# A graph attention scores pass: gather indices copied by GpSimd instead of ScalarE, and step words loaded once per engine

## The reference, as far as it matters

```
q, k, v = x @ Wq.T + bq, x @ Wk.T + bk, x @ Wv.T + bv
score[edge, head] = sum over d of q[src, head, d] * k[dst, head, d]
```

## Time and profile before

| | |
|---|---|
| median of 3 timed runs | 3451.3 us (3447.9 to 3469.26) |
| span of the profiled execution, first to last instruction | 3661.6 us |
| what lies around that span | not listed |
| granted TensorE clock, mean over the span | 0.899 |
| the scores pass in that execution | about 168 to 947 us |
| PE, DVE, ACT, POOL busy over the span | 2959.8, 2114.3, 1131.1, 1144.8 us |
| DMA over the span | 477.37 MB, mean 130 GB/s |

### The profile page before, as it was taken

How to read it: one execution, slowest core, us unless ns; L and a number is a source line. 1 busy time by engine, 2 the same in 40 slices (tenths; PEclk the granted TensorE clock), 3 DMA queues, 4 the chain that set the end, 5 groups by cost and what they waited for, 6 DMA issues and landing times. The chain is left out here.

```text
span 3661.6 us, 59295 instructions
## 1 busy us (share of the span) xinstructions
PE 2959.8 (81%) x12458; PEld 2278.7 (62%) x12459; DVE 2114.3 (58%) x4039; ACT 1131.1 (31%) x2511; POOL 1144.8 (31%) x1257
## 2 busy tenths in 40 slices
PE   3766566666289969999999799999997996667878
PEld 2633344433155537777776688888886885555677
DVE  6356555555689754434522465656667995885521
ACT  1010111100188723333333000000004994655412
POOL 3155555555022110000000455555552002760033
PEclk9877787866599989999999899999998998998979
DMA  1587777777377610000000665656662114005334
GB/s 47 176 251 218 213 226 224 225 227 223 90 228 226 181 70 1 1 8 8 5 4 8 202 192 173 191 173 188 191 188 67 44 44 153 1 1 183 101 130 136
DMA packets 259676, 477.37 MB, mean 130 GB/s; under 512 B 31340, under 2 KB 148020, under 8 KB 258156
## 3 DMA queue, kind: packets, MB, share of 16 engines
q1 hardware_dynamic: 198510, 282.91, 24.4%
q0 software_dynamic: 61056, 193.06, 18.4%
HBM read 376.68 MB, written 100.16 MB: 130 GB/s over the span
## 5 line engine op out<-in xcount | busy, mean ns | idle before, releaser
L1664 PE MATMUL bank<-conv_w,conv_eT 128*128 128x256 f32 x2520 | 579.7, 380 | 0.0
L1605 POOL DMA_INDIRECT conv_h<-table_h,conv_ix x424 | 416.3, 982 | 339.0 <-ACT conv_ix L1594 191.1
L1664 PEld LDWEIGHTS bank<-conv_w,conv_eT 128*128 128x128 f32 x2520 | 480.2, 191 | 65.8
L557 POOL DMA_INDIRECT x<-table_qv,scores_ix x324 | 307.2, 948 | 393.1 <-ACT scores_ix L505 280.8
L579 PE MATMUL bank<-scores_k,scores_hotT 128*128 x864 | 327.7, 518 | 53.3 <-issue 48.7
L1397 ACT ACTIVATE area<-bank,nodes_bi,nodes_sc 128x320 f32<-128x320 f32 x320 | 197.6, 617 | 373.9 <-PE bank L1314 373.9
L579 PEld LDWEIGHTS bank<-scores_k,scores_hotT 128*128 128x128 f32 x864 | 205.6, 258 | 136.6 <-issue 105.2
L571 PE MATMUL bank<-lines,pick 128*128 x216 | 74.8, 346 | 256.3 <-DVE scores_hotT L662 150.8
L1545 DVE SCALAR_TENSOR_TENSOR x<-bank,nodes_w,x 128x256 f32<-128x256 f32 x200 | 96.6, 484 | 319.9 <-PE bank L1323 319.9
L505 ACT ACTIVATE scores_ix<-src 128x2 int32 x216 | 43.8, 203 | 727.1 <-DVE scores_qk L669 429.0
L1045 PE MATMUL bank<-attend_pv,rows 128*128 128x260 f32 x864 | 237.9, 405 | 36.7 <-DVE attend_pv L1026 21.5
(11 more groups left out here) (449 smaller groups left out, 5445.7 us busy)
## 6 DMA issues: line engine op xcount, KB each, us to landing
conv_eT<-in_edges SPq DMA_DIRECT2D x212, 384.0 KB
attend_v<-edge_v SPq DMA_DIRECT2D x216, 256.0 KB, 3.0
edge_v<-x SPq DMA_DIRECT2D x162, 256.0 KB
edge_v<-scores_qv SPq DMA_DIRECT2D x54, 256.0 KB
hidden_rows<-top_wide SPq DMA_DIRECT2D x25, 512.0 KB, 3.2
projected<-spline_hst SPq DMA_DIRECT2D x10, 960.0 KB, 4.5
ball_hT<-projected SPq DMA_DIRECT2D x5, 1920.0 KB, 17.3
top_wd<-in_top_wd SPq DMA_DIRECT2D x8, 1024.0 KB, 13.7
```

The lines of the kernel that those rows point to most:

```text
L557: nc.gpsimd.indirect_dma_start(out=qv(u)[:, g - u * G, :], out_offset=None, in_=m.d_qv, in_offset=bass.IndirectOffsetOnAxis(ap=ix[:, g:g + ...
L1605: nc.gpsimd.indirect_dma_start(out=h[:, u, g, :], out_offset=None, in_=m.d_h, in_offset=bass.IndirectOffsetOnAxis(ap=ix[:, u * G + g:u * G ...
L1664: mm = nc.tensor.matmul(banks[u][:, g * F:(g + 1) * F], eT[:, u, g, c], w[:, c], start=c == 0, stop=c == EC - 1)
```

## The change

The index copy moves from ACT to POOL. POOL now loads and decodes the step's word itself, waits for the free slot, copies the indices, waits for its own copy, and issues the gathers. ACT keeps only the copies for the projection and the context and one new wait (for its own exponentials).

On PE and DVE each step's word is loaded once and kept in registers until its second use: PE keeps 4 words, DVE 3, carried from round to round (`carried`, `words`). The node tile and the edge tile are decoded where they are used, and only the one that is used; SP and POOL decode only the edge tile. DVE drops three waits: for `k_made` before the one-hot, for `reduced` before the product, and for `scored` before the reduction.

```diff
             @block.scalar
-                act.sem_inc(freed, RING)
-                def sources(r, u):
-                    s = act.snap(r * RING + u)
-                    t, i = step_at(act, m, s)
-                    act.wait_ge(freed, s + 1)
-                    nc.scalar.activation(ix[:, u * G:(u + 1) * G], m.src[:, bass.ds(i, G)], ACT.Copy).then_inc(index, 1)
...
                 with act.Fori(0, FIRST) as n:
-                    for u in range(RING):
-                        sources(n + 1, u)
-                        if u % 2:
-                            j = u // 2
-                            act.wait_ge(product, n * 4 + (j + 1))
+                    for j in range(2 * FT):
+                        act.wait_ge(product, n * 4 + (j + 1))
...
+                act.wait_ge(exps, FT)
                 with act.Fori(0, SECOND) as n:
+                    for u in range(2):
+                        take_tile(n * 2 + u)
+                        keep_front(n * 2 + u, u)
...
             @block.gpsimd
+                pool.sem_inc(freed, RING)
                 with pool.Fori(0, rounds_of(pool, m, RING)) as r:
                     for u in range(RING):
-                        pool.wait_ge(index, r * RING + (u + 1))
+                        s = pool.snap(r * RING + u)
+                        i = edge_tile(pool, word_at(pool, m, s))
+                        pool.wait_ge(freed, s + 1)
+                        nc.gpsimd.tensor_copy(ix[:, u * G:(u + 1) * G], m.src[:, bass.ds(i, G)]).then_inc(index, 1)
+                        pool.wait_ge(index, s + 1)
                         pool.wait_ge(stored[u], r * 16 + 16)
...
             @block.tensor
-                def spread_out(r, u):
-                    t, i = step_at(pe, m, r * RING + u)
+                def spread_out(r, u, word):
+                    i = edge_tile(pe, word)
...
-                def keys(r, u):
-                    t, i = step_at(pe, m, r * RING + u)
+                def keys(r, u, word):
+                    t = node_tile(pe, word)
...
+                def round_of(r, words, between):
+                    for u in range(RING):
+                        keys(r, u, words[u])
+                        words.append(word_at(pe, m, r * RING + (u + KEPT)))
...
             @block.vector
-                def one_hot(r, u):
-                    t, i = step_at(dve, m, r * RING + u)
+                def one_hot(r, u, word):
+                    t = node_tile(dve, word)
                     dve.wait_ge(spread, r * RING + (u + 1))
-                    dve.wait_ge(k_made, r * RING + (u + 1))
...
-                    dve.wait_ge(reduced, r * RING + (u + 1))
...
+                        if more or u + 3 < RING:
+                            words.append(word_at(dve, m, r * RING + (u + 3)))
...
-                    dve.wait_ge(scored, r * RING + (u + 1))
...
-                    t, i = step_at(dve, m, r * RING + u)
```

More of the change, by code:

```diff
@@ L625, in _ @@
                 with pe.Fori(0, SECOND) as n:
[L626 to L634, removed]
+                    for x, word in zip(carried, round_of(n + (FIRST + SHIFT), [pe.snap(x) for x in carried], lambda u: mixing(n, u))):
+                        pe.reg_mov(x, word)
+                rounds(FIRST + SHIFT + SECOND, last)
                 front(NT - 1)
+                words = [pe.snap(x) for x in carried]
                 for u in range(RING):
-                    keys(last, u)
+                    keys(last, u, words[u])
+                    if u + KEPT < RING:
+                        words.append(word_at(pe, m, last * RING + (u + KEPT)))
                     if u + UN - 1 < RING:
-                        spread_out(last, u + UN - 1)
+                        spread_out(last, u + UN - 1, words[u + UN - 1])
                 back(NT - 1, 0)
@@ L684, in _, with round_of @@
-                last = last_round(dve, m, RING)
-                for u in range(2):
-                    t, i = step_at(dve, m, u)
-                    dve.wait_ge(spread, u + 1)
-                    nc.vector.tensor_scalar(hotT[:, u % UN], numbers(u), m.node[:, bass.ds(t, 1)], None, ALU.is_equal).then_inc(hots, 1)
-                with dve.Fori(0, FIRST + 1) as r:
-                    for u in range(RING):
-                        score(r, u, True)
+                def round_of(r, words, more):
+                    for u in range(RING):
+                        for g in range(u * G, (u + 1) * G):
+                            dve.wait_ge(gathered[g], r * 16 + 16)
+                        dve.wait_ge(k_made, r * RING + (u + 1 + UN))
+                        nc.vector.tensor_tensor(qk[:, u % 2].rearrange("p (g f) -> p g f", g=G), qv(u)[:, :, 0:F],
+                                                banks[u % UN][:, 0:G * F].rearrange("p (g f) -> p g f", g=G), ALU.mult).then_inc(freed, 1)
+                        if more or u + 3 < RING:
+                            words.append(word_at(dve, m, r * RING + (u + 3)))
+                        if u + 2 < RING:
+                            one_hot(r, u + 2, words[u + 2])
+                        elif more:
+                            one_hot(r + 1, u + 2 - RING, words[u + 2])
+                        i = edge_tile(dve, words[u])
+                        dve.wait_ge(freed, r * RING + (u + 1 + RING))
+                        nc.vector.tensor_reduce(dot[:, u % 2], qk[:, u % 2].rearrange("p (g h d) -> p g h d", g=G, h=HEADS),
+                                                AX.X, ALU.add).then_inc(reduced, 1)
+                        dve.wait_ge(reduced, r * RING + (u + 3))
+                        dve.wait_ge(scored, r * RING + (u + 2))
+                        at = m.scores[:, :, bass.ds(i, G)]
+                        nc.vector.tensor_tensor(at, at, dot[:, u % 2].rearrange("p g h -> p h g"), ALU.add).then_inc(scored, 1)
+                    return words[RING:]
@@ new lines, in rounds @@
+                def rounds(begin, end):
+                    with dve.Fori(begin, end) as r:
+                        for x, word in zip(carried, round_of(r, [dve.snap(x) for x in carried], True)):
+                            dve.reg_mov(x, word)
+                last = last_round(dve, m, RING)
+                carried = [dve.alloc_register(f"scores_word{j}") for j in range(3)]
+                for u in range(3):
+                    word = word_at(dve, m, u)
+                    dve.reg_mov(carried[u], word)
+                    if u < 2:
+                        one_hot(0, u, word)
```

85 lines of the change are left out of this document (29 added, 56 removed).

## The result

| | before | after |
|---|---|---|
| median of 4 runs each, us | 3456.11 (3447.9 to 3469.26) | 3602.91 (3599.96 to 3629.96) |
| ratio | 1 | 1.0437 (95% interval 1.0407 to 1.0467) |
| span of the profiled execution, us | 3661.6, again 3452.1 | 3598.3 |

The change makes the kernel 4.4% slower, 146.8 us between the medians. Forecast were 3581 us, within 3425 to 3640. One timed execution of the kernel before, taken beside the first experiments, lasted 14303 us; why is not known, and no ratio here counts it.

A forecast was written before the change was run, and what follows sets the result against it. Untraced, POOL's gathers were taken to be close to the pace of the scores pass. That pass going from 604 to 734 us cost 130, all other parts 0: 3451.3 + 130 = 3581 us, range 3425 to 3640.

The forecast's parts named there:

- the sequencer can't issue the next gather until the copy is done: Scores pass: POOL's queue runs empty once a step; 0.83 us from copy end to the gather that waited.
- asked for as a sign: Profile after: pairs of gathers 1.25 us apart, successive pairs 3.3; DVE's waits for gathers from 25 us to a hundred or more.
- The cycle: POOL's step in the scores pass after the change: 3.22 us plus a gap of 0 to 0.30, taken as 3.30.
- The tail: Scores pass after the change: 21 us from the last gather to the stage's end.
- The pass before: Untraced scores pass before the change: 569 to 734 us, taken as 604 with five sixths of the trace's surplus in it.
- DVE at 2.2 us a step is quicker: Scores pass before the change: DVE's 2.2 us a step is under POOL's 2.50, so POOL is close to the pace.
- The span: Profiled execution after the change: 3620 to 3720 us, as DVE's slowed steps already take longer than POOL's 3.3.
- The edits at nothing: ACT's lost copies, DVE's and PE's single loads, the dropped waits and SP's fewer decodes: 0 us each.
- A: Rival: DVE's slow stretches in the scores pass are real and hide POOL's 3.3 us; 3440 us, no change; chance 0.17.
- B: Rival: word loads cause DVE's issue gaps in the scores pass, making it 78 us shorter; 3373 us; chance 0.13.
- C: Rival: same mechanism, 0.30 us gap before the copy, whole surplus in the scores pass; 3663 us; chance 0.05.
- D: Rival: POOL's sequencer queues gathers behind the copy without waiting; cycle 2.8 us, cost 22 us, 3473 us; chance 0.07.

The follow-up runs named there:

- e1: The kernel before with only the index copy moved to POOL, words still loaded twice: 3595.54 us, ratio 1.0387; run again, 3594.66 us.
- e4: The changed kernel with POOL copying the next step's indices before issuing this step's gathers: 3457.68 us, ratio 1.0019 to the kernel before.
- e2: The changed kernel with the index copy back on ACT, sparing loads and dropped waits kept: 3443.52 us, ratio 0.9971 to the kernel before; again, 0.9988.
- e7: The changed kernel with POOL copying two steps' indices, waiting once, then issuing four gathers: 3530.75 us, ratio 1.0212 to the kernel before.
- e3: The changed kernel with gathers reading a table filled once, each copy waited for eight steps later: 3447.8 us, ratio 0.9978 to the kernel before.
- e6: The kernel before plus one 128x25 operation per step on DVE, between the reduction and the add: 3455.65 us, ratio 1.0006.
- after_again: The changed kernel, unaltered, run a second time: 3613.45 us, ratio 1.0438 to the kernel before.

## Why the prediction was right

**The mechanism holds.** The step "the sequencer can't issue the next gather until the copy is done" is shown from both sides: e1 has the whole loss of the pass without the other edits, e4 with the copy but without waiting for a fresh one loses 13.7 us of gathers against e2 where after loses 163.9, and e7 with half the waits loses half. What was asked for as a sign is there: pairs of gathers 1.28 apart, successive pairs 3.26 to 3.27 apart, no longer run, and 203.3 us of waits for gathers on DVE.

**The cycle.** Forecast was 3.22 us and a gap, taken as 3.30. The gap before the copy is nothing (gather 302.72 + 0.95, copy 303.68), the other terms 0.03 to 0.04 more, and the typical cycle 3.26. That the mean is 3.300 all the same is luck: it comes from four steps of 4.85 to 4.87 us and from 3.32 to 3.34 at the end of most rounds, which I hadn't thought of. 0.83 from the earlier trace rows, a single row of a different releaser, is the price again (0.83, 0.84, and 0.89 at times).

**The tail was mis-sized.** "21 behind the last" was carried over from before, where the ring was full and DVE up to eight steps behind the gathers. A starved DVE follows closely: from the last gather (881.3) to 2.7 us behind the last product's start (889.3), which is where the pass ended at 947 in the first profile, are 10.7 us. The pass after is 724 us, not 734.

**The pass before was mis-sized.** "I put five sixths of the surplus in this pass, so 604." By the same ends it is 583 us (168 to 751): all but 14 us of the 210.3 sat in it, and the bound of 569 was nearer than my value. The cost in the pass is 724 - 583 = 141 us for the forecast 130. With 6 us in the next stage that I had at nothing, the difference is 147, as measured. The remaining 5 of the 22 us between 3581 and 3602.9 are the medians of before themselves, 3451.3 and 3456.1. The sum of 561 us for this pass came to 22 us too little because it had POOL's gathers follow each other without a stop. "DVE at 2.2 us a step is quicker" is the reading behind it, and it wasn't borne out: 2.2 is one of the shortest steps, and the mean in the undisturbed profile is 2.58. This did no harm to the forecast, as POOL's 3.26 is slower than either.

**The span was wrong.** I expected 3620 to 3720 for the profiled execution, from the reading "that the trace hides it behind a slowed DVE". Span and timed runs agree within 2 us in every later profile (3598.3 us of an execution of 3599.96, and 3452.1 of 3453.79). The slow register instructions belonged to that one execution. That they weren't the kernel's usual pace was right; that every profile brings them was not, as no later one has such a surplus. What brought them is open.

**The edits at nothing.** ACT's relief shows no gain: e1 and e4 have it, and neither is faster than before. The sparing loads bring 14 us in the pass where POOL can use them (e2) and none beside the waiting POOL (711.0 in e1, 710.8 in after), as "with POOL at 3.3 us a step DVE and PE have a microsecond to spare" says. POOL's own load is hidden, though it isn't 0.3 us but 0.62 in the median: the copy still starts as the gather ends. The Trainium skill (DMA: Bandwidth & Descriptors, section Latency and other measured facts) gives about 600 ns as the floor of a register load. By that rule an exposed load a step would cost 130 us, an estimate from the page's figure; on POOL beside gathers the median of 622 ns is close to it, though its shortest load took 283 ns, and on DVE (304 ns in the median) the trace contradicts it. As POOL's load isn't exposed here, neither changes the sum.

**The rivals.** A (the slow stretches are real, 3440) fell with the first run: the second profile of before has none. That DVE's pace mattered to the kernel before, the other half of A, is nearer the truth than I allowed: most of the 22 us that POOL stood still are a full ring. B (the loads are the stall, 3373) fell with e2, though the same edits gave 14 us of gathers. C (3663) had the pass before nearly right (569 for 583), and the wrong gap. D (the sequencer doesn't wait) is refuted by the 0.83 us; its cycle, 2.8, would even then have been 2.58, as e3 and e4 show.

**Slowness of the engine.** POOL's copy lasts 193 ns in the median here, ACT's 0.20 us. By the preference for other engines in the Trainium skill (Perfetto Trace Analysis, section Optimizing GPSIMD Operations) the loss would be put down to a slow engine. The runs here contradict it: e4 keeps all the copies on POOL and its median can't be told from that of before, so here the order and the wait decide, not the engine.

## What to carry to other kernels

Where an engine has to wait for its own last instruction before it may issue the next, count the wait and not only the instruction; here it cost 0.68 us each time, over three times the 0.19 of the copy itself. If an engine has to produce its own operands, let it produce those of the next step ahead of this step's work (e4): here the gathers then took 14 us longer than without the copy, instead of 164. An operation added to test whether an engine is a bound must not fall into a time in which that engine waits anyway; look in the timeline where it lies (e6). Before a surplus in one traced execution is divided among stages, look whether a second one has it.

## What was not expected of the hardware

- A 128x2 copy queued between two indirect DMAs costs 0.08 us, not its 0.19: it lies in the 0.30 us of idle time between two gathers.
- From the end of a copy to the gather that waits for it are 0.83 us on the same engine, and 0.15 us if nothing has to wait.
- In one execution of the kernel before, a register instruction on DVE took up to 728 ns; in the next profile it never took more than 45, and 195 us less lay between the first and the last gather.
- A register load on POOL takes 0.62 us in the median beside its gathers (283 to 1039 ns), half of that on DVE, and 288 ns in the median on POOL itself in the next stage, where it issues no gathers.
- In the next stage a POOL copy of 128x8 that starts while DVE multiplies 128x512 ends only behind it: 0.25 or 0.48 us instead of 0.19, by how much of the product was left. The index copies of the scores pass, where DVE's product reads a bank, never took more than 209 ns in after, and at most 233 in after_again.
